# Cutting a fused attention and expert layer's loads and stores into smaller transfers

## The reference

```
xn = layernorm(x)                                   # x: (2, 8192, 1024) fp32
x  = x + attention(xn) + moe(xn)
attention: 16 query heads, 4 key/value heads of 64, rotary, ALiBi, softmax over 8192 keys, @ Wo
moe: 8 experts of width 768 (gated SiLU), top 2 of a softmax gate, and a shared MLP of width 1536
```

## Time and profile before

| | us |
|---|---|
| median of 2 runs | 4408.63 (4407.6 to 4409.66) |
| profiled execution, its time | 4409.54 |
| its span (core 2, the slowest) | 4407.9 |
| spans of the 8 cores | 4396.6 to 4407.9 |
| 16 DMA engines, mean rate over the span | 31 GB/s |

### The profile page before, as it was taken

One profiled execution on the slowest core, in us unless ns is written; L12 is line 12 of the kernel. 1 busy time (PEld: TensorE's weight loads), 2 busy tenths in 40 slices (PEclk: granted clock), 3 DMA queues, 4 the chain that ended last, 5 costly groups with the idle time before them and its releaser, 6 DMA issues. The chain is left out here.

```text
span 4407.9 us, 37114 instructions; the slowest of 8 cores (4396.6 to 4407.9 us)
## 1 busy us (share of the span) xinstructions
PE 3063.8 (70%) x12536; PEld 1145.6 (26%) x12536; DVE 1251.4 (28%) x1819; ACT 1435.9 (33%) x1561; POOL 21.4 (0%) x29
## 2 busy tenths in 40 slices
PE   3333333222778888967888988599999999999811
PEld 1111111111112222221122222244444444444311
DVE  4555555553210000022000000133233332322333
ACT  1111111110557788935578986000100001000000
POOL 0000000000000000000000000000000000000000
PEclk7556655555778899987689999799999999999955
DMA  3111111112000000000000000521202212020033
GB/s 77 48 55 48 43 56 52 34 34 38 0 0 1 1 1 1 1 39 0 1 1 1 1 1 17 107 43 29 43 15 43 43 29 43 15 44 1 10 114 105
DMA packets 63911, 136.16 MB, mean 31 GB/s; under 512 B 4456, under 2 KB 26984, under 8 KB 63728
## 3 DMA queue, kind: packets, MB, share of 16 engines
q0 software_dynamic: 22432, 52.45, 6.9%
q1 hardware_dynamic: 41296, 81.34, 5.9%
HBM read 169.43 MB, written 16.78 MB: 42 GB/s over the span
## 5 line engine op out<-in xcount | busy, mean ns | idle before, releaser
L67 ACT ACTIVATE PT_B<-PS_B,alibi_sb 128x1024 bf16<-128x1024 f32 x626 | 694.0, 1109 | 398.6 <-PE PS_B L67 398.3
L67 PE MATMUL PS_B<-Qpair,K 64*128 64x512 bf16 x1252 | 425.5, 424 | 163.3 <-ACT PT_B L67 142.9
L67 ACT ACTIVATE PT_A<-PS_A,alibi_sb 128x1024 bf16<-128x1024 f32 x428 | 476.5, 1113 | 101.4 <-PE PS_A L67 72.9
L67 PE MATMUL PA<-xn,w1sb 128*128 128x512 bf16 x1920 | 442.9, 391 | 31.1 <-DVE wbc L67 27.8
L67 PE MATMUL PVB<-PT_B,V 128*65 128x512 bf16 x1252 | 427.2, 427 | 0.0
L67 PE MATMUL TP<-id_sb,xntm 128*128 128x128 bf16 x640 | 80.9, 307 | 496.1 <-DVE xntm L67 362.6
L67 PE MATMUL PB<-xn,w1sb 128*128 128x512 bf16 x1920 | 424.2, 379 | 0.0
L67 ACT ACTIVATE gact<-PA 128x1024 f32<-128x1024 f32 x60 | 61.4, 1023 | 875.6 <-PE PA L67 875.6
L67 ACT ACTIVATE lns<-vvs,eps_sb 128x1 f32<-128x1 f32 x80 | 23.5, 294 | 828.3 <-DVE vvs L67 828.3
L67 PE MATMUL PVA<-PT_A,V 128*65 128x512 bf16 x856 | 273.7, 402 | 10.9 <-ACT PT_B L67 10.9
L67 PE MATMUL PS_A<-Qpair,K 64*128 64x512 bf16 x856 | 270.3, 398 | 5.0 <-ACT PT_A L67 4.7
(11 more groups left out here) (121 smaller groups left out, 2389.2 us busy)
## 6 DMA issues: line engine op xcount, KB each, us to landing
xt<-xb SPq DMA_DIRECT2D x64, 512.0 KB, 3.7
w1sb<-w1t POOLq DMA_DIRECT2D x10, 3072.0 KB, 19.8
w2sb<-w2t POOLq DMA_DIRECT2D x10, 1536.0 KB, 11.2
xt<-xown SPq DMA_DIRECT2D x16, 512.0 KB, 3.6
zacc<-zst SPq DMA_DIRECT2D x16, 512.0 KB, 2.7
zin<-zacc SPq DMA_DIRECT2D x16, 512.0 KB, 4.8
xtb<-xown SPq DMA_DIRECT2D x16, 512.0 KB, 5.6
out<-osb SPq DMA_DIRECT2D x16, 512.0 KB, 3.2
```

Source lines behind the costliest of these rows:

```text
L67: ins = getattr(e, m)(*a, **kw)
```

## The change

Six DMA statements are cut along the free dimension into loops of 2 or 4 DMAs, each with a part of the same bytes to the same place, on the same queue and semaphore. Nothing else moves.

- Stage A, `xt`: 4 DMAs of 256 columns (1,024 bytes a partition) in place of one.
- Stage C, `w1sb`: 2 DMAs of four of the eight 128-row groups; `w2sb`: 2 DMAs of three of the six. At the head of the stage and in the loop.
- Stage D, `zin`: 2 DMAs of four of the eight 512-byte pieces; `xtb` and `out`: 4 DMAs of 256 columns each.

```diff
-            r.op("sync", "dma_start", xt[:, tb:tb + 1024], src_r[:, lt, :], inc=[(sxp, 16)])
+            for ch in range(4):
+                r.op("sync", "dma_start", xt[:, tb + ch * 256: tb + (ch + 1) * 256],
+                     src_r[:, lt, ch * 256:(ch + 1) * 256], inc=[(sxp, 16)])
...
-            r.op("gpsimd", "dma_start",
-                 w1sb[:, buf * 12288:(buf + 1) * 12288].rearrange("p (dc f) -> p dc f", dc=DC),
-                 w1_d[e + 2].rearrange("(dc p) f -> p dc f", p=128), inc=[(gw[buf], 16)])
+            for ch in range(2):
+                r.op("gpsimd", "dma_start",
+                     w1sb[:, buf * 12288 + ch * 6144: buf * 12288 + (ch + 1) * 6144]
+                     .rearrange("p (dc f) -> p dc f", dc=4),
+                     w1_d[e + 2].rearrange("(dc p) f -> p dc f", p=128)[:, ch * 4:(ch + 1) * 4, :],
+                     inc=[(gw[buf], 16)])
...
-        r.op("sync", "dma_start", zin[:, bb:bb + 1024].rearrange("p (dc c) -> p dc c", dc=DC),
-             z_r[:, :, tb * 128:(tb + 1) * 128], inc=[(s4p, 16)])
-        r.op("sync", "dma_start", xtb[:, bb:bb + 1024], xo_r[:, tb, :], inc=[(s4p, 16)])
+        for ch in range(2):
+            r.op("sync", "dma_start",
+                 zin[:, bb + ch * 512: bb + (ch + 1) * 512].rearrange(
+                     "p (dc c) -> p dc c", dc=4),
+                 z_r[:, ch * 4:(ch + 1) * 4, tb * 128:(tb + 1) * 128], inc=[(s4p, 16)])
+        for ch in range(4):
+            r.op("sync", "dma_start", xtb[:, bb + ch * 256: bb + (ch + 1) * 256],
+                 xo_r[:, tb, ch * 256:(ch + 1) * 256], inc=[(s4p, 16)])
...
-        r.op("sync", "dma_start", out_d[tb * 128:(tb + 1) * 128, :], osb[:, bb:bb + 1024],
-             inc=[(so[tb % 2], 16)])
+        for ch in range(4):
+            r.op("sync", "dma_start", out_d[tb * 128:(tb + 1) * 128, ch * 256:(ch + 1) * 256],
+                 osb[:, bb + ch * 256: bb + (ch + 1) * 256], inc=[(so[tb % 2], 16)])
```

More of the change, by code:

```diff
@@ L860, in build_nc @@
         buf = e % 2
-        r.op("gpsimd", "dma_start",
-             w1sb[:, buf * 12288:(buf + 1) * 12288].rearrange("p (dc f) -> p dc f", dc=DC),
[L863 to L866, removed]
+        for ch in range(2):
+            r.op("gpsimd", "dma_start",
+                 w1sb[:, buf * 12288 + ch * 6144: buf * 12288 + (ch + 1) * 6144]
+                 .rearrange("p (dc f) -> p dc f", dc=4),
+                 w1_d[e].rearrange("(dc p) f -> p dc f", p=128)[:, ch * 4:(ch + 1) * 4, :],
+                 inc=[(gw[buf], 16)])
+        for ch in range(2):
+            r.op("gpsimd", "dma_start",
+                 w2sb[:, buf * 6144 + ch * 3072: buf * 6144 + (ch + 1) * 3072]
+                 .rearrange("p (hc c) -> p hc c", hc=3),
+                 w2_d[e].rearrange("(hc p) c -> p hc c", p=128)[:, ch * 3:(ch + 1) * 3, :],
+                 inc=[(gw[buf], 16)])
         dg_w[e] = gw[buf].v
@@ L973, in build_nc @@
             r.wait("gpsimd", T, t_eo_done[e])
-            r.op("gpsimd", "dma_start",
-                 w2sb[:, buf * 6144:(buf + 1) * 6144].rearrange("p (hc c) -> p hc c", hc=6),
-                 w2_d[e + 2].rearrange("(hc p) c -> p hc c", p=128), inc=[(gw[buf], 16)])
+            for ch in range(2):
+                r.op("gpsimd", "dma_start",
+                     w2sb[:, buf * 6144 + ch * 3072: buf * 6144 + (ch + 1) * 3072]
+                     .rearrange("p (hc c) -> p hc c", hc=3),
+                     w2_d[e + 2].rearrange("(hc p) c -> p hc c", p=128)[:, ch * 3:(ch + 1) * 3, :],
+                     inc=[(gw[buf], 16)])
             dg_w[e + 2] = gw[buf].v
```

## The result

| us | before | changed |
|---|---|---|
| executions compared (5 and 6) | 4408 to 4413 | 4431 to 4473 |
| profiled execution, its time | 4409.54 | 4455.81 |
| its span, slowest core | 4407.9 (core 2) | 4454.3 (core 5) |
| spans of the 8 cores | 4396.6 to 4407.9 | 4413.8 to 4454.3 |

The ratio is 1.0084, with a 95% interval of 1.0043 to 1.0125: 0.84% slower, some 37 us, where 9 us (0.2%) were forecast; 4408.6 x 1.0084 is 4446 us, above the forecast range of 4405 to 4440. Both are within 2% of before.

The account below looks back on a forecast made before the run. No stage was taken as bound by DMA bandwidth; stage D's serial load path counted. Stage D +7.7, stage A +1.5 and stage C 0 us gave +9.2, so 4418 us; range 4405 to 4440 us.

Parts of the forecast that it names:

- All of the change in stage D, nothing in stages A and C: Whole kernel: stage D +7.7 us; stage A hidden but for +1.5 us at its start; stage C 0.
- The 5.5 us of slack before VectorE waits: Stage A loop: an `xt` load could slip 5.5 us before VectorE waits; quarters slip it at most 1.5 us, cost 0.
- the 1.7 us of ScalarE: Stage A loop: by ScalarE's own clock too, the quarters' slip of at most 1.5 us stays inside 1.7 us.
- 1.5 forecast: Stage A start: first tile waits for its load while GpSimd's weight loads share the engines; +1.5 us, between +0.2 and +1.9.
- The load path of 6.47 us a tile: Stage D's serial loop of 14.76 us: 6.47 us from the store's issue to the landing of `xtb`.
- So the later issue just fits under the store's transfer: Stage D: `zin` issued at 1.72 us, first packet about 2.5; store's data through at 2.5 to 2.9, so no cost.
- the sign that the prediction itself named for exposed issues: Stage D, profile after: gaps in the DMA engines between store and `zin` would show the forecast wrong.
- covered by 1.1 us: Stage D: last `xtb` quarter could end at 5.1 us, against 5.8 + 0.45 us the packets need anyway.
- +0.45 us a tile for packets and completions: Stage D: +0.20 for the store, +0.20 for `xtb`, under 0.1 us for seven more completion packets.
- the free case: Rival, stage D: finer pieces hide the 0.6 us start-up a tile and balance the packets; 4405 to 4411 us, chance 0.14.
- The rival of exposed issues: Stage D: SP becomes the clock, held at each issue behind a half of `zin`; +2.9 us a tile, 4455 us, chance 0.14.
- The transfers go in turn: Rival: pieces of one queue do not overlap; `xt` 6.0 us late 80 times, 4,890 us or more, chance 0.03.

## Why the prediction was wrong

- *All of the change in stage D, nothing in stages A and C*: right. The 5.5 us of slack before VectorE waits held for 79 tiles; the 1.7 us of ScalarE did not always hold (26 further waits on core 5), which cost nothing. At the start the first tile began 0.5 us later in the mean of the cores (21.6 for 21.1), against 1.5 forecast, and none of it reached stage D. TensorE's wait at the head of stage C was 37.6 us in the mean of the cores, after 37.8 before.
- *The load path of 6.47 us a tile is what counts*: right; it became 7.45 in the tile shown and 7.56 in the median of core 7.
- *"So the later issue just fits under the store's transfer"*: this step failed. It took `zin`'s first packet 0.8 us after its issue, at 2.5 us, just behind the store's data. The 0.8 us is what the store at the head of the loop shows; `zin`, issued at 1.90, had its first packets 1.24 us later, at 3.14, and the store's data were through at 2.8 to 2.9. The engines ran dry between the two, which is the sign that the prediction itself named for exposed issues. The term stood at 0 in the sum; with the store alone cut it was the whole +0.75 us a tile.
- *"The last quarter of `xtb` is issued at 9 x 0.43 = 3.9 us, could start at 4.7 and end at 5.1 ... covered by 1.1 us"*: the numbers are low, but the cover was there. The nine issues took 4.43 us, 0.49 each, and with 1.24 to the first packet and 0.4 of data the piece could have ended at 6.1, where the last packets ended at 7.3. With all of stage D but `zin` cut, this issue came 0.45 us earlier and the landing did not.
- *+0.45 us a tile for packets and completions*: not seen on the path. As engine time the term is +0.18 on core 7 (4.95 to 5.13), made of two parts that the prediction had as +0.20 each: in the packet records `xtb` in quarters costs 0.35 us more (1.35 to 1.71), but the store 0.2 less (1.76 to 1.56), since its slow start shrank, as the free case had it. With loads and store in two queues none of it reached the period. What reached it, 1.05 us, came of the issues, so that 0.45 was too low by 0.6: 9 us of the missing 28.
- *The rival of exposed issues*, 4455 us at 0.14: right in kind, but a third of its price a tile, and by another way: SP was held for at most 0.13 us longer than usual behind the halves of `zin` and not for a microsecond at each piece, and what was exposed was the start of the loads. That its time agrees with that of the profiled execution, 4455.81, is luck: the slowest core there has the 2.5 us a tile more of a pair in step.
- *Not foreseen at all*: two cores in step slowing each other. It makes the slowest core, on which the metric rests: 1.05 x 15 = 16 us on every core, and up to 2.5 x 15 = 38 us more on the worst pair. This is the larger part of the miss. The forecast reasoned from one core. No row of before told of it: its pairs all ran stage D 2.4 us or more apart.
- *The transfers go in turn*: excluded, as forecast. This bears also on the Trainium skill, DMA: Bandwidth & Descriptors, "Anatomy of one DMA", whose fixed 2 us a DMA are given there for DMAs issued from GpSimd. On SP's queue no such sum is paid piece by piece: the four quarters of a store, issued 0.4 to 0.5 us apart, landed 0.5 us apart, each 1.75 to 1.92 us after its issue (core 7).

What stays open: what divides the half microsecond behind the gap, and why halves of `zin` keep two cores in step. A whole `zin` could let one core's read go first and put the other behind by its length, where halves alternate; the distance at which whole transfers settle, 2.6 to 3.3 us, is near `zin`'s own transfer, but this is only argued. It is also not shown that whole transfers in the serial loop would leave a collision as those with early loads do.

## What to carry to other kernels

In a serial loop whose loads stand behind a store in one queue, compare two times: when the data of the store are through, and when the first load's first packet can come, which is all the issues ahead of it plus the time from its issue to its first packet, measured on a load. If the second is later, the engines run dry, and cutting the store costs that gap in every pass. The piece that lands last need not be the late one: look at what the engines do between its issue and its landing. Cutting cost nothing where nobody stood behind the queue. A period that differs from pair to pair, but not within a pair, was here a sign of cores in step: compare their timelines before looking for a cause in the program. Here the cure was order, not size: whole loads issued ahead of the store took 100 us off in the two executions whose cores all reached stage D in time.

## What was not expected of the hardware

- The first packets of `zin` came 1.24 us after its issue, with the engines running dry; those of the store at the head of the loop came 0.8 us after its issue.
- The store in quarters took less engine time than whole (1.56 us a tile for 1.76), the residual's load in quarters more (1.71 for 1.35).
- Two cores of a pair that ran the same loop in step had both a period of 17.5 to 18.1 us, to within 0.1 us of each other, where pairs 5 us or more apart had 15.6.
- The issues of a tile on SP stand 0.49 us apart in place of 0.43; with the loads issued from a second queue, the cut loop is as fast as the whole one.
